# Edge tiles of 127 instead of 128, a reordered prologue and written-out layers in a graph network kernel

## The reference, cut to what matters

```
h = relu(layernorm(x)) @ enc_w + enc_b ;  h_list = [h]
for l in 0..2:
    e   = edge_attr @ edge_w[l] + edge_b[l]            # 212500 x 128
    msg = relu(h[src] + e)                             # rows of h gathered by edge
    agg = segment_sum(msg, dst)                        # 12500 x 128
    z   = (1 + eps[l]) * h + agg
    h   = relu(relu(z @ w1[l] + b1[l]) @ w2[l] + b2[l]);  h_list.append(h)
out = x + concat(h_list) @ out_w + out_b
```

## Time and profile before

| what | value |
|---|---|
| median of 3 runs | 6340.28 us |
| the profiled execution | 6351.8 us |
| its span, first to last instruction | 6350.0 us |
| GpSimd busy | 4751.3 us (75%) |
| TensorE busy | 4765.8 us (75%) |
| VectorE busy | 1817.2 us (29%) |
| ScalarE busy | 981.1 us (15%) |
| mean granted TensorE clock | 0.573 of full speed |

### The profile page before, as it was taken

One profiled execution on the slowest core, in us unless ns is written; L12 is line 12 of the kernel. 1 busy time (PEld: TensorE's weight loads), 2 busy tenths in 40 slices (PEclk: granted clock), 3 DMA queues, 4 the chain that ended last, 5 costly groups with the idle time before them and its releaser, 6 DMA issues.

```text
span 6350.0 us, 67297 instructions
## 1 busy us (share of the span) xinstructions
PE 4765.8 (75%) x14494; PEld 2936.8 (46%) x14495; DVE 1817.2 (29%) x4231; ACT 981.1 (15%) x1582; POOL 4751.3 (75%) x5075
## 2 busy tenths in 40 slices
PE   7877777777777777777777777777777777777777
PEld 5544444444444444444444444444444444444444
DVE  6322222222222222222222222222222222222222
ACT  4111111111111111111111111111111111111111
POOL 6777777777777677777777777767777777777776
PEclk8655555555555555555555555555555555555555
DMA  4222222222222222222222222222222222222223
GB/s 133 65 63 63 61 63 63 63 62 60 63 63 63 61 61 63 63 63 63 63 63 63 61 63 63 63 59 61 63 63 63 61 63 63 63 63 63 63 63 97
DMA packets 254393, 412.87 MB, mean 65 GB/s; under 512 B 107879, under 2 KB 160438, under 8 KB 253734
## 3 DMA queue, kind: packets, MB, share of 16 engines
q0 software_dynamic: 159456, 326.88, 19.9%
q1 hardware_dynamic: 52893, 64.81, 3.6%
q10 hardware_dynamic: 42000, 20.75, 1.2%
HBM read 379.85 MB, written 32.25 MB: 65 GB/s over the span
## 4 chain that ended last, share of the span: by engine, by line
POOL 49%; issue 17%; PE 15%; DMA 11%; DVE 4%; ACT 3%; POOLq 1%; DVEq 0%; SPq 0%; ACTq 0%
POOL rows L324 49%; DMA rows<-h_table,idx 11%; PE bank L561 10%; PE bank L555 3%; DVE rows L817 3%; ACT rows L478 3%; PE bank L580 0%; PE bank L533 0%; PE bank L582 0%; POOLq L208 0%; PE bank L525 0%; DMA h_table<-rows 0%; POOLq L209 0%; DVE onehot L682 0%; DMA out_acc<-x_t 0%
## 5 line engine op out<-in xcount | busy, mean ns | idle before, releaser
L324 POOL DMA_INDIRECT rows<-h_table,idx x4983 | 4714.3, 946 | 1556.0 <-issue 1292.0
L561 PEld LDWEIGHTS bank<-onehot,rows 128*128 128x128 f32 x9966 | 2085.3, 305 | 2961.5 <-ACT rows L478 2564.3
L561 PE MATMUL bank<-onehot,rows 128*128 128x64 f32 x9966 | 2234.8, 399 | 1522.9 <-ACT rows L478 1483.6
L555 PE MATMUL bank<-edgew,attr 65*128 x2496 | 2230.1, 1006 | 12.9 <-issue 8.2
L817 DVE TENSOR_TENSOR rows<-bank,rows 128x512 f32<-128x512 f32 x1248 | 861.9, 691 | 3868.3 <-DMA rows<-h_table,idx 3805.8
L478 ACT ACTIVATE rows<-rows 128x512 f32<-128x512 f32 x1248 | 784.6, 629 | 5260.0 <-DVE rows L817 5260.0
L555 PEld LDWEIGHTS bank<-edgew,attr 65*128 65x128 f32 x2496 | 660.6, 308 | 272.3 <-issue 272.2
L804 DVE TENSOR_TENSOR onehot<-bank,dst_rel 128x256 f32<-128x256 f32 x1248 | 526.8, 422 | 168.7 <-issue 154.3
L813 DVE TENSOR_TENSOR agg_t<-bank,agg_t 128x64 f32 x1248 | 281.0, 225 | 425.0 <-issue 223.5
L580 PE MATMUL bank<-agg_t,w1s 128*128 (+1 forms) x150 | 149.2, 1098 | 4.7 <-DVE agg_t L813 4.7
L588 PE MATMUL bank<-hid,w2s 128*128 128x512 f32 x300 | 145.1, 607 | 0.0
(11 more groups left out here) (80 smaller groups left out, 469.1 us busy)
## 6 DMA issues: line engine op xcount, KB each, us to landing
rows<-h_table,idx POOLq DMA_INDIRECT x4983, 2.5
attr<-ea_t SPq DMA_DIRECT2D x156, 256.0 KB, 3.8
h_table<-h_n ACTq DMA_DIRECT2D x72, 256.0 KB, 2.5
out<-out_acc SPq DMA_DIRECT2D x25, 256.0 KB, 3.2
h_table<-rows SPq DMA_DIRECT2D x24, 256.0 KB, 2.3
out_acc<-x_t SPq DMA_DIRECT2D x4, 1280.0 KB, 18.5
idx<-src_t SPq DMA_DIRECT2D x156, 16.0 KB
rows<-dst_g SPq DMA_DIRECT2D x1, 832.0 KB
```

Source lines behind the costliest of these rows:

```text
L324: return g.indirect_dma_start(dst, None, h_table[l % 2], bass.IndirectOffsetOnAxis(ap=index, axis=0))
L555: return nc.tensor.matmul(dst[:, 0:tiles * D], cols, edgew[:, bass.ds(l, 1), 0:tiles * D].rearrange("p a n -> p (a n)"), start=True, stop= ...
L561: last = nc.tensor.matmul(dst[:, 0:WIN], rows[:, slot, j, :], onehot[:, hot_slot, j, :], start=(j == 0), stop=(j == tiles - 1))
```

## The change

A tile has 127 edges (`EP`), so a layer has 1,674 tiles in 419 groups, the last with two tiles. Every edge-side buffer and operation covers partitions 0 to 126. The indices of all tiles lie in one buffer that is loaded once in the prologue. GpSimd's program is written out in full, as are the layers on every engine; the bodies stay a loop on TensorE, VectorE and ScalarE. The parts of x from the third on are issued by ScalarE, the dst loads and the small parameters by SyncE between the stores of h. The order of nodes within a unit changes, so that a partition stores 4 rows that lie together in the table. The last layer leaves out the transposes, `h_n`, the seed of a following layer and the store. VectorE loads the bases of 8 groups at once. The waits of `window_sums` on `hot` and `added` and of `e_terms` on `summed`, and of `one_hot` on `agg_done`, go.

The core of the diff:

```diff
+EP = 127
-        idx = [sb(f"idx{i}", [P, HB * TG], i32) for i in range(4)]
+        idx = sb("idx", [P, NTE], i32)
         # SyncE
-            for part in range(NPARTS):
-                load_x(part)
-                if part == 2:
-                    sp.dma_start(dst_n, dst_g.rearrange("c (g e) -> c g e", g=GR)).then_inc(s_dst, 16)
-            sp.dma_start(dst_i, dst_t).then_inc(s_dst_t, 16)
+            for part in range(2):
+                load_x(sp, part)
...
+                made = p_rows[i % 4].rearrange("p t d -> p (t d)")
+                    sp.dma_start(h_units[0][:, i, :], made).then_inc(p_stored[i % 4], 16)
+                if i == 8:
+                    sp.dma_start(dst_n, ...)
+                if i == 10:
+                    sp.dma_start(dst_i, dst_t).then_inc(s_dst_t, 16)
+                if i == 12:
+                    sp.dma_start(idx[0:EP, :], src_t).then_inc(idx_in, 16)
...
         # GpSimd
-                            wait_apart(g, agg_done, c * (4 * HB) + (l * NG + r * HB + k + S0 - RING + 1))
-                            for j in range(tiles):
-                                gather(l, rows[:, slot, j, :], idx[r][:, k * TG + j:k * TG + j + 1])\
-                                    .then_inc(gathered[slot], 16)
-                with g.Fori(0, NB // 4 - 1) as c:
-                    edge_bodies(c, 0)
-                edge_bodies(NB // 4 - 1, SPARE)
+                for group in range(NG):
+                    slot = group % RING
+                    if l == 0 and group == 0:
+                        g.wait_ge(idx_in, 16)
+                    if l == 0 and group == HB:
+                        g.wait_ge(s_ready, 1)
+                    if l or group >= RING:
+                        g.wait_ge(agg_done, l * NG + group + 1 + S0 - RING)
+                    tiles = min(TG, NTR - group * TG)
+                    for t in range(group * TG, group * TG + tiles):
+                        gather(l, rows[0:EP, slot, t % TG, :], idx[0:EP, t:t + 1]).then_inc(gathered[slot], 16)
         # ScalarE
+            for part in range(2, NPARTS):
+                load_x(act, part)
...
-                store(i)
+                    if l < L - 1:
+                        store(i)
         # TensorE
-            with pe.Fori(0, L) as l:
+            for l in range(L):
+                    cols = by_tile(h_t[:, 0:tiles * P], tiles)
+                    if l < L - 1:
+                        for j in range(tiles):
+                            last = nc.tensor.transpose(zt_ps[:, j * P:(j + 1) * P], cols[:, j, :], ident[:, :])
+                        last.then_inc(tr_done, 1)
-                        wait_apart(pe, summed, body * RING + (k - NE_PS + 1 + S0))
-                        pe.wait_ge(hot, body * RING + (k + 1))
-                        pe.wait_ge(added, body * RING + (k - NA_PS + 1 + S0))
         # VectorE
-            with dve.Fori(0, L) as l:
+            for l in range(L):
-                        base = load_base(base_row, b * RING + k)
+                        base = dve.snap(bases[k], min_val=0, max_val=NP)
+                            dve.load(bases[half * HB:(half + 1) * HB], base_row[0:1, bass.ds(b * RING + half * HB, HB)])
-                            dve.wait_ge(agg_done, body * RING + (k + 1 + S0 - NHOT))
-                            one_hot(k % NHOT, iota_ps, b * RING + k, tiles).then_inc(hot, 1)
+                        one_hot(k % NHOT, iota_ps, b * RING + k, tiles)
+                        if k >= 2:
+                            accumulate(k - 2)
```

More of the change, by code:

```diff
@@ L272, in far_pass, with load_attr @@
                         take(sp, f_next, 1)
[L273 to L285, removed]
+                        sp.dma_start(far_idx[0:EP, :], src_t[:, bass.ds(g * TG, TG)]).then_inc(f_idx, 16)
+                        sp.dma_start(attr[0][0:KA - 1, 0:EP], ea_t[:, bass.ds(g * EP, EP)]).then_inc(f_attr, 16)
+                def load_attr(body, half):
+                    sp.dma_start(attr[half][0:KA - 1, :], ea_t[:, bass.ds((body * 2 + half) * (HB * EP), HB * EP)])\
+                      .then_inc(attr_in[half], 16)
+                sp.wait_ge(e_done, l * NG + S0)
+                load_attr(0, 0)
+                load_attr(0, 1)
+                with sp.Fori(1, NFULL) as c:
+                    for half in range(2):
+                        sp.wait_ge(e_done, c * RING + (l * NG + half * HB + S0 - HB))
+                        load_attr(c, half)
+                for half in range(-(-REST // HB)):
+                    sp.wait_ge(e_done, NFULL * RING + l * NG + half * HB + S0 - HB)
+                    load_attr(NFULL, half)
                 far_passes(sp, load_extra(sp), far_pass)
-            with sp.Fori(0, NU) as i:
+            with sp.Fori(0, ND) as i:
                 sp.wait_ge(o_added, i + ((L - 1) * NU + 1 + N0))
@@ L468, in node_body, with edge_body @@
                     relu_h(i)
-                    store(i)
[L471 to L486, removed]
+                    if l < L - 1:
+                        store(i)
+                def edge_body(b, groups):
+                    for k in range(groups):
+                        half, kk = k // HB, k % HB
+                        if kk == 0 and groups - k >= HB:
+                            unit = load_unit(act, b * 2 + half)
+                        tiles = real_tiles(b, k)
+                        act.wait_ge(summed, b * RING + (l * NG + k + 1 + S0))
+                        part = rows[0:EP, k, 0:tiles, :]
+                        nc.scalar.activation(part, part, ACT.Relu).then_inc(relued, 1)
+                        if kk in (2, 3, 5)[:3 if l < L - 1 else 2] and groups - half * HB >= HB:
+                            with act.If(unit > 0):
+                                (relu_z if kk == 2 else relu_h if kk == 3 else store)(unit_before(unit))
+                with act.Fori(0, NFULL) as b:
+                    edge_body(b, RING)
+                edge_body(NFULL, REST)
                 first = load_left(act)
@@ new lines, in sums @@
+                        window_sums(agg_ps[k % NA_PS], k, k % NHOT, real_tiles(b, k)).then_inc(agg_done, 1)
+                    for k in range(min(2, groups)):
+                        e_terms(k)
+                    for k in range(groups):
+                        half, kk = k // HB, k % HB
+                        if kk == 0 and groups - k >= HB:
+                            unit = load_unit(pe, b * 2 + half)
+                        if k + 2 < groups:
+                            e_terms(k + 2)
+                        sums(k)
+                        if kk in (1, 2, 3) and groups - half * HB >= HB:
+                            with pe.If(unit > 0):
+                                if kk == 1:
+                                    wait_apart(pe, added, first_group + (half * HB + S0))
+                                    node_z(unit_before(unit))
+                                elif kk == 2:
+                                    node_h(unit_before(unit))
+                                else:
+                                    node_out(unit_before(unit))
@@ L815, in add_terms @@
             def add_terms(slot, ps, tiles=TG):
-                part = rows[:, slot, 0:tiles, :]
-                return v.tensor_tensor(part, ps[:, 0:tiles * D].rearrange("p (t d) -> p t d", d=D), part, ALU.add)
+                part = rows[0:EP, slot, 0:tiles, :]
+                return v.tensor_tensor(part, ps[0:EP, 0:tiles * D].rearrange("p (t d) -> p t d", d=D), part, ALU.add)
             def far_pass():
@@ L868, in accumulate @@
                         add_window(base, agg_ps[k % NA_PS]).then_inc(added, 1)
-                    for half in range(2):
-                        unit = load_unit(dve, b * 2 + half)
-                        for kk in range(HB):
-                            k = half * HB + kk
-                            tiles = GL if last and k == RING - 1 else TG
-                            dve.wait_ge(agg_done, body * RING + (k + 1 + S0 - NHOT))
-                            one_hot(k % NHOT, iota_ps, b * RING + k, tiles).then_inc(hot, 1)
-                            dve.wait_ge(e_done, body * RING + (k + 1 + S0))
-                            dve.wait_ge(gathered[k], body * (16 * TG) + 16 * TG)
-                            add_terms(k, e_ps[k % NE_PS], tiles).then_inc(summed, 1)
-                            if k >= 2:
-                                accumulate(k - 2)
-                            if kk == 4:
-                                with dve.If(unit > 0):
-                                    node_take(unit_before(unit))
@@ L885, in edge_body @@
-                    accumulate(RING - 2)
-                    accumulate(RING - 1)
-                with dve.Fori(0, NBODY - 1) as b:
-                    edge_body(b, False)
-                edge_body(NBODY - 1, True)
+                    for k in range(groups):
+                        half, kk = k // HB, k % HB
+                        if kk == 0:
```

(33 more changed lines are left out.)

250 lines of the change are left out of this document (127 added, 123 removed).

## The result

The changed kernel takes 14542.24 us (median of 4 runs, 14541.08 to 14543.01) against 6340.29 us for the kernel before (median of 4, the three runs given above and one more); ratio 2.2935, 95% interval 2.2907 to 2.2963. The forecast was 5,290 us with a range up to 6,400.

What follows compares the result with a forecast made beforehand. GpSimd's preparing of gathers was taken as the bound: 5,173 us for gathers + 121 + 11 - 8 + 3 - 1 = 5,299 of span, about 5,290 us at the median (-16.6%); range 3,690 to 6,400.

Steps and rivals of the forecast that it cites:

- What bounds the kernel: How fast GpSimd can prepare gathers bounds the kernel: 4,983 gathers, one every 1.25 us, 6,229 us of the span.
- Price of a gather: GpSimd's gather of 127 rows falls from 0.947 to 0.72 us, 1.03 with its gap; 5,173 us in all.
- the rival's 4.06: Time for one engine to drain a gather's 32 packets; a generator waiting for each would need 4.06 us a gather.
- The one share itself: 127 rows, a prime count, go to one DMA engine as one share instead of 16 shares of 8 rows.
- Landing: One engine drains a gather in 4.06 us instead of 0.25; hidden except at three layer ends, +11 us.
- Prologue: Before the first gather, stores of h no longer queue behind x and dst: -8 us, bounds -12 and 0.
- First ring: The first 64 gathers fill the ring in 66 us instead of 80, then GpSimd waits: +3 us.
- TensorE's clock: TensorE falls behind at the lower clock level, is granted the upper, catches up; does not bound while the ring absorbs it.
- rivals C and D: C: gathers at 0.40 to 0.70, work behind binds, 3,330 us, chance 0.17; D: TensorE at lower clock, 5,685 us, 0.08.
- Rival B: At GpSimd's line 324 the generator waits for one engine's drain: 20,400 us, half 10,200; decides above 1.242 us; chance 0.13.
- Rival A: The gather's price goes with its rows, so 127 save almost nothing: 6,344 us, no change, or 6,380; chance 0.14.
- The rest of the change: Written-out program, one index buffer and dropped waits give nothing, since neither loop nor index waits cost GpSimd anything.

Runs made afterwards that it cites:

- a_ep128: The changed kernel with EP = 128 and nothing else undone, so tiles, loads and gathers of 128; 6327.88 us, ratio 0.9979 to the kernel before.

## Why the prediction was wrong

*What bounds the kernel* was right: line 324 and nothing else, a gather every duration plus 0.30 us. The count of 5,022 was right, and so was the account by which 1 us a gather is 5,022 us of the span.

*Price of a gather* is the step that failed. It took the 0.947 us as half rows, half shares and let the share half shrink when one share is left: 0.72 us. Measured: 2.548 us. 5,022 x (2.848 - 1.03) = 9,130 us, the whole error of 9,252 us but 120. Two things in it were wrong. The fixed part is neither rows nor shares: 64 rows, half of them, still take 0.900. And fewer shares are not less work: by their packets, the engines that take no part are given as many filler descriptors as the share has rows, so one share of 127 is 2,032 descriptors instead of 128, and the price rose with that number, with 120 rows as the exception. The chosen value lay between a lower bound from a memset of 0.09 us and the row of 0.947, both on the cheap side of the rival's 4.06; that no row held another row count should have kept the likeliest value near the only one measured, with the direction open.

*The one share itself* was right, though the packets were misread on the way: 2,050 B is the mean of 16 packets of 4,096 B, eight rows each, and 16 completions of 4 B, and not the size of 32 packets of four rows. The rule in the Trainium skill ("DMA: Bandwidth & Descriptors", the section on why a DMA increments its semaphore by 16) agrees with this case at every count tried: 16, 15, 14, 5, 2 and 1 shares for 128, 120, 126, 125, 122 and 127 rows are its largest divisors up to 16. The uneven 16 shares that it tells of for some direct copies don't occur in these gathers.

*Landing*: 7.6 us from issue instead of the 6.3 worked out, from 2.5. Of the 5.1 more, 1.6 are the dearer making; from its end to the landing it is 5.1 us instead of 1.6, 3.5 more, near the forecast's 3.8. The closeness is in part luck, since the drain of 4.06 us behind it was too long: the rows of one share start over some 2.5 us. It stayed hidden except at the ends of layers, where the prediction had +11 us. Changes of layer and tail grew by 30.8; in the kernel with tiles of 127 and gathers of 128 they are 9.6 us shorter, about what the landings make. The rest is the second unit, which the prediction missed in moving from 416 groups to 419.

*Prologue*: for gathers of 128 rows -6.5 us, within the bounds, near the -8. In the changed kernel +65.5 us. The step counted the queue that loads were moved from and not what the moved loads had become: of 127 partitions, two of them, in front of the stores. Each of these loads of 841 KB kept the stores behind it back for some 30 us, at a DMA share of 0.06, and padding to 128 removed it; the load of 106 partitions added 13.3 us. By the rule of the Trainium skill (same page and section) 127 partitions go to one engine on this queue too, and the share of 0.06 agrees.

*First ring, TensorE's clock, rivals C and D*: with a dear gather none of it arises; GpSimd waited 0.3 us for TensorE in the whole run. Of these nothing is tested.

*Rival B* had the right side and the right place, and its point of decision, 1.242 us, was passed; its mechanism was wrong. The generator doesn't wait for the drain: a gather lands 7.6 us after issue and the next one starts to be made after 2.85, and late landings do not make it longer. Of its times 20,400 us was far off, and 10,200, from a wait for half of the drain, 30% below the measured one. *Rival A* is what happens for counts that divide well: 112 rows, sixteen shares of 7, took 923 ns.

*The rest of the change*: written-out program, one index buffer, fewer waits left the gap at 0.30, as forecast; with 128 rows (a_ep128) a gather with its gap costs what it did, to 2 ns.

## What to carry to other kernels

Choose a gather's row count by its largest divisor up to 16, and price it by 16 times the rows of a share: here, for rows of 512 B, 0.85 us + 0.7 to 0.84 ns x 16 x share. Fewer rows can be several times dearer, and rows saved within whole sixteens save almost nothing, so fill the tile and pad the last one with valid indices. When a tile height changes, check every load that takes it as its partition count, and how many groups and units are left over at the end.

## What the runs showed of the hardware that was not expected

- Idle DMA engines get fillers in a gather: 240 packets for one of 127 rows, together the bytes of 1,905 descriptors of 4 B; 61 rows cost 1,657 ns, 128 rows 944.
- 120 rows cost 979 ns and 128 rows 944 with the same 128 descriptors; one engine is idle in the first. Why that adds some 33 ns is open.
- No row count tried takes away the last 0.85 us or so of a gather, and 0.30 us lies between any two. What it consists of is open.
- How a share of one engine is placed (in turn or not) is open: the packet records name no engine.
